# A two-layer transformer kernel: rows rounded a turn sooner in the first feed-forward, projections and square sums in another order in the attention, four banks for the router's first transposes

## The reference

```python
x = x + cross_attention(_layernorm(x), ctx)    # one head, softmax(q k^T / sqrt(512)) v, output projection
x = x + bit_ffn(_layernorm(x))                 # below
x = x + grouped_attention(_layernorm(x), ctx)  # 16 heads of 128, 4 key/value heads, rms-normed q and k
x = x + moe_ffn(_layernorm(x))                 # below

# bit_ffn: each linear rounds its input row to 8 bits and its weight to -1, 0, 1
def bit_linear(x, w, b):
    gamma_x = clip(max(abs(x), axis=-1), 1e-05, None)
    x_dq = clip(round(x * 127.0 / gamma_x), -128.0, 127.0) * gamma_x / 127.0
    return einsum('bsd,hd->bsh', x_dq, ternary(w)) + b
out = bit_linear(silu(bit_linear(x, gate)) * bit_linear(x, val), out_w, out_b)     # 512 -> 2048 -> 512

# grouped_attention
q = rmsnorm(x @ Wq + bq) * qn_w;  k = rmsnorm(ctx @ Wk + bk) * kn_w;  v = ctx @ Wv + bv
out = softmax(q k^T / sqrt(128)) v @ Wo

# moe_ffn: 8 experts of width 352, the two best of each row, and a shared expert of width 704
probs = softmax(x @ router_w.T);  topk_w, topk_idx = top_k(probs, 2);  topk_w /= sum(topk_w)
out = sum_e weight_e * (silu(x @ gw_e) * (x @ uw_e) @ dw_e) + (silu(x @ sg + bg) * (x @ su + bu)) @ sd + bd
```

## Time and profile before

| | |
|---|---|
| median of 3 runs | 1797.34 us |
| profiled execution | 1796.16 us, span 1794.4 us |
| mean granted clock of TensorE | 0.989 |
| PE busy | 1708.2 us (95%) |
| DVE busy | 1237.1 us (69%) |
| ACT busy | 925.6 us (52%) |
| POOL busy | 593.6 us (33%) |
| DMA | 238.27 MB, mean 133 GB/s |

### The profile page before, as it was taken

The page is one execution under the profiler, slowest core; times in us unless marked ns, Lnnn a source line. Parts: engine busy times, 40 slices in busy tenths (PEclk is TensorE's granted clock), DMA queues, the critical chain, the costliest instruction groups (busy, mean ns, idle before and its releaser), DMA issues. The chain is left out here.

```text
span 1794.4 us, 26446 instructions
## 1 busy us (share of the span) xinstructions
PE 1708.2 (95%) x9562; PEld 1392.6 (78%) x9582; DVE 1237.1 (69%) x2313; ACT 925.6 (52%) x1774; POOL 593.6 (33%) x469
## 2 busy tenths in 40 slices
PE   7999998996999979999999999999799999999998
PEld 6998997773444558888888788888577799999876
DVE  5444442896888768887888788888547567677555
ACT  4433432654565576676666666666231355656411
POOL 3111143223687531222231222121210255555342
PEclk9999999998999999999999999999899999999999
DMA  8223211853233671123222212210251579798573
GB/s 316 95 83 106 71 49 39 301 202 104 59 71 94 164 227 60 60 87 102 89 62 87 83 60 83 68 52 1 77 221 49 175 258 294 254 306 259 189 244 111
DMA packets 175566, 238.27 MB, mean 133 GB/s; under 512 B 51271, under 2 KB 112455, under 8 KB 173255
## 3 DMA queue, kind: packets, MB, share of 16 engines
q1 hardware_dynamic: 156620, 203.14, 34.5%
q0 software_dynamic: 9600, 33.30, 5.9%
q10 hardware_dynamic: 9216, 0.14, 0.3%
HBM read 184.24 MB, written 43.78 MB: 127 GB/s over the span
## 5 line engine op out<-in xcount | busy, mean ns | idle before, releaser
L1233 POOL TENSOR_TENSOR a_rq<-a_ssq,a_qhalf 128x4 f32<-128x4 f32 x64 | 65.3, 1021 | 360.4 <-DMA a_ssq<-a_sum_row 360.4
L78 PE MATMUL bank<-a_xT_hi,a_wq_lo 128*128 128x512 f32 (+1 forms) x384 | 143.3, 373 | 1.4 <-DVE a_xT_lo L503 1.4
L80 PE MATMUL bank<-a_xT_hi,a_wq_hi 128*128 128x512 f32 (+1 forms) x384 | 138.1, 360 | 0.0
L79 PE MATMUL bank<-a_xT_lo,a_wq_hi 128*128 128x512 f32 (+1 forms) x384 | 137.4, 358 | 0.0
L78 PE MATMUL bank<-a_wo_hi,a_oT_lo 128*128 128x512 f32 x320 | 127.4, 398 | 7.5 <-issue 2.7
L1396 ACT ACTIVATE a_scores<-a_scores,a_nmax 128x256 f32<-128x256 f32 x256 | 126.9, 512 | 0.8 <-DVE a_nmax L1571 0.8
L79 PE MATMUL bank<-a_wo_lo,a_oT_hi 128*128 128x512 f32 x320 | 126.4, 395 | 0.0
L80 PE MATMUL bank<-a_wo_hi,a_oT_hi 128*128 128x512 f32 x320 | 126.3, 395 | 0.0
L2111 POOL TENSOR_TENSOR e_wg_lo<-raw_g,e_wg_hi 128x1408 fp32r<-128x1408 f32 x25 | 87.9, 3514 | 112.4 <-ACT e_wg_hi L2183 112.4
L1385 ACT ACTIVATE a_sum_row<-bank,a_sum_eps 1x512 f32<-1x512 f32 x64 | 43.4, 678 | 141.0 <-PE bank L1759 140.6
L1273 POOL TENSOR_TENSOR f_h<-f_vv,f_gs 128x512 f32<-128x512 f32 x64 | 93.2, 1460 | 61.7 <-DVE f_vv L1501 61.0
(11 more groups left out here) (423 smaller groups left out, 5402.3 us busy)
## 6 DMA issues: line engine op xcount, KB each, us to landing
raw_g<-in_egw SPq DMA_DIRECT2D x26, 704.0 KB, 4.7
raw_u<-in_euw SPq DMA_DIRECT2D x26, 704.0 KB, 6.2
a_xT_hi<-x1T_hi SPq DMA_DIRECT2D x16, 1024.0 KB, 6.2
a_xT_lo<-x1T_lo SPq DMA_DIRECT2D x16, 1024.0 KB, 8.4
raw_d<-in_edw SPq DMA_DIRECT2D x26, 512.0 KB, 5.8
y_routed<-m_y SPq DMA_DIRECT2D x39, 256.0 KB, 6.3
raw_d<-in_edw SPq DMA_DIRECT2D x26, 192.0 KB, 7.0
a_cTraw<-in_ctxT SPq DMA_DIRECT2D x8, 512.0 KB, 5.6
```

What stands on the lines that cost most here:

```text
L78: pe.matmul(out, w[1], x[0], start=first, stop=False)
L79: pe.matmul(out, w[0], x[1], start=False, stop=False)
L80: return pe.matmul(out, w[0], x[0], start=False, stop=last)
L1233: pool.tensor_tensor(rq[:, h % HG, :], ssq[u % 2][:], qhalf[:], ALU.pow).then_inc(s_rq, 1)
```

## The change

Five edits, of order alone: no instruction is added or left out on any engine, and no DMA.

1. First feed-forward: `norm` of tiles 4 to 7 and `quantised_x(2)`, `(3)` stand ahead of DVE's loop, `round_x(2)`, `(3)` ahead of ACT's; from turn 1 on a turn rounds and quantises tile `n + 3` and not `n + 2`. Later groups are normed in turns 3 and 7 (before: 4 and 8), their maximum and scales and POOL's product follow a turn sooner.
2. Attention, PE: `square_sums` stand behind `output(u)` in turns 0 to 3 and in the late turns (elsewhere they stay ahead of it); at the start `next_xT(T - 1)` goes ahead of `square_sums(2)`, and `queries(3)` ahead of turn 0's transposes.
3. Attention, turns 62 and 63: heads 0 and 1 of `project_last` go ahead of `project(u)`.
4. Router: the first four transposes have a bank each; DVE's list has the four norms, the four `transposed`, then the next four norms; inside the loop the norms of a chunk stand together behind the fourth `transposed`.
5. Router: the last six operations of `first_groups` are a function of their own (`bases`), behind `shared_hidden(M + 2)`; `add(4)`, `add(5)` stand ahead of `experts_of_groups`, `add(8)`, `add(9)` ahead of `row_columns(3)`.

```diff
                 for j in range(NH):
-                    if j == 1 and n % GT == 2 and n // GT + 1 < len(GROUPS):
+                    if j == 1 and n % GT == 1 and n // GT + 1 < len(GROUPS):
                         product_scales(n // GT + 1)
...
+            round_x(2)
             xT_copy(0)
             xT_copy(1)
+            round_x(3)
             for n in range(T):
...
-                if n + 2 < T:
-                    round_x(n + 2)
+                if n and n + 3 < T:
+                    round_x(n + 3)
...
+            for t in range(*GROUPS[1]):
+                norm(t)
+            quantised_x(2)
+            quantised_x(3)
             for n in range(T):
-                g, i = n // GT + 1, n % GT
+                g, i = (n + 1) // GT + 1, (n + 1) % GT
...
-                if n + 2 < T:
-                    quantised_x(n + 2)
+                if n and n + 3 < T:
+                    quantised_x(n + 3)
...
+            next_xT(T - 1)
             square_sums(2, 2)
-            next_xT(T - 1)
             for u in range(G * U):
                 g, i, n = u // U, u % U, u // HG
+                late = i == HG and g
+                if u == 0:
+                    queries(3)
                 transposed(u, n, i)
-                if u + 3 < G * U:
+                if u and u + 3 < G * U:
                     queries(u + 3)
                 if u + 2 < G * U:
                     scores(u + 2)
-                if u == G * U - 2:
-                    pe.wait_ge(s_masked, G * U * CT)
-                late = i == HG and g
+                if u >= G * U - 2:
+                    if u == G * U - 1:
+                        pe.wait_ge(s_masked, G * U * CT)
+                    for k in range(HG - 2):
+                        project_last(range(k, k + 1), range(CT // 2) if u == G * U - 2 else range(CT // 2, CT))
                 if n and not late:
                     project(u)
-                if u >= G * U - 2:
-                    project_last(range(HG - 2), range(CT // 2) if u == G * U - 2 else range(CT // 2, CT))
-                if u + 3 < G * U:
+                    if u + 3 < G * U:
+                        square_sums(u + 3, i + 3)
+                output(u)
+                if (late or not n) and u + 3 < G * U:
                     square_sums(u + 3, i + 3)
-                output(u)
                 if late:
                     project(u)
...
+        rows_bank = lambda t: yb[t - 2] if t in (2, 3) else tb[t % 2]
...
+                return c, e
+
+            def bases(a, c, e):
                 step(dve.tensor_tensor(e[:], c[:], groups[:], ALU.subtract))
...
-            norm(0)
+            for t in chunk(0):
+                norm(t)
             dve.wait_ge(s_rw, 1)
             dve.tensor_tensor(rw2[:, :, E:2 * E], rw[:], f32(rw2[:, :, 0:E]), ALU.subtract).then_inc(s_rw, 1)
-            for t in range(1, CT):
+            for t in chunk(0):
+                transposed(t)
+            for t in chunk(1):
                 norm(t)
...
-                if m + 1 < M:
-                    norm(t + CT)
-                    norm(t + CT + 1)
...
-                    norm(t + CT + 2)
-                    norm(t + CT + 3)
+                    for later in chunk(m + 2):
+                        norm(later)
...
-            ends = first_groups(a)
+            ends, starts = first_groups(a)
             shared_hidden(M + 2)
-            experts_of_groups(ends)
+            bases(a, ends, starts)
             add(4, 4)
             add(5, 5)
+            experts_of_groups(ends)
...
+            add(8, 8)
+            add(9, 9)
             row_columns(3)
-            for t in chunk(2):
-                add(t, t)
+            add(10, 10)
+            add(11, 11)
...
                 pe.wait_ge(s_xn, t + 1)
-                if t >= 2:
+                if t >= CT:
                     pe.wait_ge(tr.lo, t - 1)
```

More of the change, by code:

```diff
@@ L2202, in transposed @@
                 act.activation(xc[t // CT].hi[:, :, t % CT * P:(t % CT + 1) * P],
-                               tb[t % 2][:].rearrange("p (k s) -> p k s", k=KD), ACT.Copy).then_inc(tr.hi, 1)
+                               rows_bank(t)[:].rearrange("p (k s) -> p k s", k=KD), ACT.Copy).then_inc(tr.hi, 1)
             def logit_rows(c):
@@ L2303, in transposed @@
                 cols = slice(t % CT * P, (t % CT + 1) * P)
-                dve.tensor_tensor(xc[t // CT].lo[:, :, cols], tb[t % 2][:].rearrange("p (k s) -> p k s", k=KD),
+                dve.tensor_tensor(xc[t // CT].lo[:, :, cols], rows_bank(t)[:].rearrange("p (k s) -> p k s", k=KD),
                                   f32(xc[t // CT].hi[:, :, cols]), ALU.subtract).then_inc(tr.lo, 1)
@@ L2453, in first_groups @@
                 step(dve.tensor_tensor(base[:], base[:], earlier[:], ALU.add))
-                return c
             def experts_of_groups(ends):
@@ L2633, in transpose @@
                 pe.wait_ge(s_xn, t + 1)
-                if t >= 2:
+                if t >= CT:
                     pe.wait_ge(tr.lo, t - 1)
                 for k in range(KD):
-                    last = pe.transpose(tb[t % 2][:, k * P:(k + 1) * P], xn[t % CT][:, k * P:(k + 1) * P], ident[:])
+                    last = pe.transpose(rows_bank(t)[:, k * P:(k + 1) * P], xn[t % CT][:, k * P:(k + 1) * P], ident[:])
                 last.then_inc(tr.mm, 1)
```

## The result

The changed kernel takes 1778.29 us (median of 4 runs, 1777.65 to 1780.04), the kernel before 1797.99 us (4 runs, 1795.54 to 1804.4). The ratio is 0.9883, 95% interval 0.9866 to 0.9901: faster by 1.2%. The profiled execution took 1780.04 us with a span of 1778.1, 16.3 us less than before.

What follows compares the result with a forecast made beforehand. PE was busy 95% of the span, so only its 86 us of idle time and its slow stretches could be won. Terms 2.0 + 1.3 + 5.9 + 4.65 + 5.6 = 19.5 us gave 1777.5 us, range 1768 to 1789.

Steps and rivals of the forecast that it cites:

- Edit 1, 2.0 us: First feed-forward: PE's waits for the quantised row total 8.7 us; sooner rows win 2.0 us, bounds -1 to +8.7.
- ACT's wait for the scale: First feed-forward: ACT waits 1.34 us for `f_sh` before its rounding, so PE would start sooner and then stop inside the turn.
- The rule's worst case: Turn 7, first feed-forward: four norms each wait out one POOL product, making edit 1 about zero and the sum 17.6 us.
- Edit 2, 1.3 us: Attention: 0.6 from turns 1 to 3, 1.4 at turn 4, less 0.7 at the start; late turns 0.
- the sign that I gave: Attention: first turns' waits for `a_sq_lo` shrink, while the time from turn 0 to turn 4 falls by 1 to 2 us only.
- Edit 3, 5.9 us: Attention turns 62 and 63: matmuls moved ahead fill PE's waits and avoid the low clock; bounds 4.2 to 6.1 us.
- all three pieces: Attention's end: 2.5 us of turn 62's wait filled, 1.65 us from no clock fall, 1.75 us in turn 63.
- Edit 4, 4.65 us: Router: 2.35 us from sooner low parts, 1.0 from the clock, 1.3 from the second chunk's wait; bounds 2.3 to 5.2.
- Edit 5, 5.6 us: Router additions: waits give 0.87, 2.34 and 0.8 us, the clock 1.6 us; bounds 2.5 (clock and third wait stay) to 6.2.
- the row was the only bound: Rival: first feed-forward's 8.7 us of waits for the row go whole, 6.7 us more, 1770.8 us; chance 0.15.
- The waits move on: Rival: clock stays low in three stretches, edits 1 and 2 give nothing, additions leave 2 us; 1787.4 us; chance 0.18.
- Slower: Rival: in all 16 first feed-forward turns `f_hq` takes 3.06 us instead of 1.22, adding 29.4 us; 1809 us; chance 0.04.

Runs made afterwards that it cites:

- The short maxima: Kernel before, but DVE takes the maximum over the first 128 of each 1024 columns; first feed-forward 197.97 us, one execution 1792.92 us.
- The split in quarters: Changed kernel with POOL's split of the query weight cut into four pieces in turns 6 to 9; 1778.80 us, ratio 0.9888, first feed-forward 199.88 us.
- two later kernels with the same router code: Changed kernel with square_sums(2) ahead of next_xT(T - 1) again, 1778.46 us; changed kernel with POOL's scales behind the products and query-weight split in quarters, 1771.92 us.
- the four made from it: Changed kernel with: old order at the attention's start, 1778.46 us; POOL's scales behind the products, 1774.53; query-weight split in quarters, 1778.80; both POOL moves, 1771.92.

## Why the prediction was right, and where it was not

The time was 1778.29 us for 1777.5, and no stage's gain was off by more than about 1.2 us. That the times agree to 0.8 us is in part luck: executions of the kernel before lie between 1795.54 and 1804.4 us, and the start stretch alone moves by 2.5. Point by point:

- *Only PE's idle time and its slow stretches can be won, and nothing behind takes it back*: right. PE's work is the same, and from the first routed product to the end both profiles take the same time.
- *Edit 1, 2.0 us*: the size was right (1.7 to 2.1), and partly by luck. The waits for the row went over to bank waits of nearly the same sum, as said. But I booked the four norms ahead of the loop as the edit's cost, and by themselves they bring 1.9 us. For the norms in turn 7 I had a bound of 1 us, half of 2.1; there they are 3.1 us of DVE's work (1.48 + 3 x 0.53), the turn grew from 13.6 to 15.4, and 1.8 us were lost. A gain that I had booked as a cost and a loss that I had too small came out at my net figure. I named ACT's wait for the scale as what holds the turn. The short maxima make that loop shorter by some 6 us in all (203.8 to 198.0), so it does hold the turns, but in a loop through DVE every operation of DVE counts, norms too, and not only the chain from product to scale. The split in quarters took 2.2 us off the long turn.
- By the Trainium skill, "SBUF — State Buffer", section "Who interferes with whom", VectorE's two-port operations and GpSimd's exclude each other. The runs agree for `f_hq`: 2.96 us beside the split of 4.55 us, 1.22 us when the split is in quarters. The rule's worst case, all four norms stretched, did not come: one was, and it is as long in the kernel before.
- *Edit 2, 1.3 us*: that the late turns give nothing was right; the term was mis-sized, about 2.5 us over fourteen profiles. I had left the clock out of it. The new order runs turns 0 to 3 at 0.95 to 1.00, the old at 0.88 to 0.96; at the same clock the difference is 0.7 us. That ACT's loop sets the first turns was not tested, and the sign that I gave can't be read as I meant it: turns 0 to 3 take 33.12 us for 36.20, but `queries(3)` has left them and turn 0 comes 2.35 us later.
- *Edit 3, 5.9 us*: right in size (6.2) and in all three pieces; the kernel with edit 3 alone shows no slow stretch.
- *Edit 4, 4.65 us*: right for the two waits of DVE, not for the clock. DVE's stop of 1.64 us and the two norms went out of its list, 2.6 us where I had 2.35, and the second chunk's wait of 1.3 us is gone. I took 1.0 us for products that would run at full clock sooner, because PE would hardly wait; in the changed kernel PE still waits 2.69 us for the low parts, where I had said at most 0.5, since the transposes end sooner too, and the products run at 0.50. In two later kernels with the same router code they ran at 1.00, and the two stretches took 44.7 us for 46.04: the term is 0 or about 1.4 by the way the clock falls.
- *Edit 5, 5.6 us*: right (5.87), with one left-over wait of 0.45 us where I had two of 0.2 to 0.3. By its own condition (the clock and the third wait stay) its lower bound was 0.87 + 2.34 = 3.2 us and not 2.5; the range does not hang on it.
- The rivals: *the row was the only bound* is out, since with all waits for it gone the stage gave 2.1 of 8.7 us. *The waits move on* held for edit 1 and the late turns, where the forecast had it already, and not for edits 3 and 5. *Slower*: `f_hq` beside POOL's long split took 1.7 us more than alone (1.8 before), but in one turn of sixteen, before and after.

What stays open: which piece of edit 2 in the first turns brings the 2.5 us (only the order of `square_sums(2)` was tried by itself, and it brings nothing), what the sooner rounding of edit 1 gives by itself, what decides between the start stretches of 417 and 419 us, and what decides where the slow piece at the router falls.

## What to carry to other kernels

A wait that names an operand of an in-order engine names what came last, not what was scarce: before such an operand is made sooner, ask what that engine did in front of it, and try to take that away alone. Two changes of the same sum need not be the same change: set their times side by side turn by turn. Work is cheapest where its engine waits anyway, so what can be done ahead of a loop belongs there; and a long operation on one engine that holds up another is worth cutting in pieces. When a change is worth 0.1%, cut the profiles at the same instructions and compare the stretch; to know how far a stretch scatters, use every profile that has the same code in it.

## What the runs showed of the hardware

The granted clock did not follow the length of a wait: in the changed kernel and the four made from it the router's first instructions are the same, behind the same wait of 2.85 us; two of the five had the slow piece on the transposes (0.69 over 4.9 us in one) and three on the products behind them (0.50 over 3.3 us in the changed kernel), and the second way takes about 1.4 us more in all. In the attention's first turns the old order ran at 0.88 to 0.96, with spans from 63.55 to 66.60 us, for the same code. A single profile carries such a choice, so terms of one or two microseconds that rest on the clock should be given as a range.
